# Lane attention: scores as one-pass products of 48 stacked rows, split by the projections

## What is computed

```python
def proj(x, W, bias):
    y = x @ W.T + bias
    y = y.reshape(b, s, H, dk, M)                  # H = 16 heads, dk = 16, M = 4 lanes
    return jnp.transpose(y, (0, 2, 1, 3, 4))
qh, kh, vh = proj(q, Wq, bq), proj(k, Wk, bk), proj(v, Wv, bv)

def interfere(x):
    return x + 0.1 * amp[0] * jnp.einsum('bhsdi,hij->bhsdj', x, interference)
qh, kh, vh = (interfere(qh), interfere(kh), interfere(vh))
scores = jnp.einsum('bhqdm,bhkdm->bhqkm', qh, kh) / math.sqrt(dk)
weights = jax.nn.softmax(scores, axis=3)
out = jnp.einsum('bhqkm,bhkdm->bhqdm', weights, vh)
return out @ Wo.T + bo
```

## Time and profile before

| | us |
|---|---|
| three runs | 3400.84, 3404.05, 3405.44 |
| median | 3404.05 |
| span of the profiled execution | 3398.2 |
| TensorE busy in it | 3209.0 (94%) |
| VectorE busy | 1418.4 (42%) |
| ScalarE busy | 893.4 (26%) |
| GpSimd busy | 347.8 (10%) |

### The profile page before, as it was taken

The page is one execution under the profiler, slowest core; times in us unless marked ns, Lnnn a source line. Parts: engine busy times, 40 slices in busy tenths (PEclk is TensorE's granted clock), DMA queues, the critical chain, the costliest instruction groups (busy, mean ns, idle before and its releaser), DMA issues. The chain is left out here.

```text
span 3398.2 us, 52110 instructions
## 1 busy us (share of the span) xinstructions
PE 3209.0 (94%) x20924; PEld 2468.5 (73%) x20924; DVE 1418.4 (42%) x2020; ACT 893.4 (26%) x1233; POOL 347.8 (10%) x304
## 2 busy tenths in 40 slices
PE   7999569998999989999999799999999999999999
PEld 4555437777788866666666688888888888778877
DVE  6888688872200027887786322122221212300000
ACT  3333344332211125555454211111111111200000
POOL 2000000000000012332332101011111010000000
PEclk9999779998999989999999899999999999999999
DMA  6776512212421241221221522222222223643443
GB/s 142 151 153 135 191 59 72 75 63 93 137 74 56 74 136 65 87 92 74 86 87 50 182 96 95 94 100 87 100 89 97 96 92 127 214 144 97 144 139 104
DMA packets 341895, 361.09 MB, mean 106 GB/s; under 512 B 154624, under 2 KB 261744, under 8 KB 339840
## 3 DMA queue, kind: packets, MB, share of 16 engines
q1 hardware_dynamic: 338304, 356.28, 33.3%
q10 hardware_dynamic: 3456, 2.90, 0.3%
HBM read 215.23 MB, written 135.36 MB: 103 GB/s over the span
## 5 line engine op out<-in xcount | busy, mean ns | idle before, releaser
L2338 PE MATMUL g_ps<-g_xs,g_wt 128*128 128x512 f32 x4128 | 950.4, 391 | 0.0
L2338 PEld LDWEIGHTS g_ps<-g_xs,g_wt 128*128 128x128 f32 x4128 | 775.8, 189 | 160.3
L2397 PE MATMUL g_ps<-g_wd,g_h 128*128 128x512 f32 x2016 | 464.2, 393 | 6.8 <-DVE g_act_out L2254 3.5
L2397 PEld LDWEIGHTS g_ps<-g_wd,g_h 128*128 128x128 f32 x2016 | 381.7, 190 | 88.9 <-DMA g_h<-g_hidden 4.3
L2254 DVE SCALAR_TENSOR_TENSOR g_act_out<-g_ps,g_g,g_act_out 128x512 f32<-128x512 f32 (+1 forms) x88 | 66.1, 751 | 672.8 <-ACT g_act_out L2187 672.7
L2187 ACT ACTIVATE g_act_out<-g_ps 128x512 f32<-128x512 f32 (+1 forms) x88 | 52.6, 598 | 634.4 <-PE g_ps L2338 634.4
L1345 PE MATMUL kv_gps<-kv_xh,kv_wh 128*128 128x512 f32 x512 | 202.1, 395 | 1.0 <-DVE kv_xl L1290 1.0
L1345 PE MATMUL kv_gps<-kv_xh,kv_wl 128*128 128x512 f32 x512 | 199.9, 390 | 0.0
L1345 PE MATMUL kv_gps<-kv_xl,kv_wh 128*128 128x512 f32 x512 | 199.6, 390 | 0.0
L1068 PE MATMUL f_gps<-f_xt,f_qwh 128*128 128x256 f32 x1024 | 192.1, 288 | 1.4 <-DVE f_xt L919 1.4
L2127 POOL TENSOR_TENSOR g_wt<-g_raw,g_wt 128x1024 fp32r<-128x1024 f32 x43 | 102.9, 2393 | 854.1 <-ACT g_wt L2164 854.1
(11 more groups left out here) (270 smaller groups left out, 4320.8 us busy)
## 6 DMA issues: line engine op xcount, KB each, us to landing
g_h<-g_hidden SPq DMA_DIRECT2D x176, 256.0 KB, 2.6
g_hidden<-g_h SPq DMA_DIRECT2D x84, 512.0 KB, 2.7
kv<-kv_y SPq DMA_DIRECT2D x16, 1024.0 KB, 5.6
g_down<-g_raw SPq DMA_DIRECT2D x22, 512.0 KB, 2.8
g_raw<-g_down SPq DMA_DIRECT2D x22, 512.0 KB, 4.1
g_raw<-in_L_ffn_gate_w_dram SPq DMA_DIRECT2D x21, 512.0 KB, 3.9
g_raw<-in_L_ffn_up_w_dram SPq DMA_DIRECT2D x21, 512.0 KB, 3.9
g_raw<-in_L_ffn_down_w_dram SPq DMA_DIRECT2D x21, 512.0 KB, 4.0
```

What stands on the lines that cost most here:

```text
L2338: w = pe.matmul(gps[:, c % 2, m, :], wt[m][i][:, l, ks], xs[c][:, r, k, :], start=(k == 0 and a == 0), stop=(k == NK - 1 and a == 2))
L2397: w = pe.matmul(to, tile[:, p % RING, l, cols], wd[f][:, r, os], start=(f == 0 and a == 0), stop=False)
```

## The change

The high part and the rest of keys and queries are made once, in `projections`, and stored so that the lane attention can load them as stacked rows. For a head and a lane there are 48 rows: of the query (high, high, rest), of the key (high, rest, high), 16 each. Their product over the 48 rows is the sum of high by high, high by rest and rest by high, one fp32r matmul of 48 rows by 128 columns for each of the eight score matrices of a chunk, four in each half of the array. Zeroed rows of other lanes are not needed, so `a_km` and GpSimd's work on it go, and so does the tile `um` from which it was made.

In `projections` ScalarE's result of a key chunk is the high part, VectorE makes the rest (`key_rest`). SyncE stores each half of a key block (eight batches) with six DMAs: high, rest, high, each as two of 64 partitions (the two heads), 256 KB in pieces of 512 B. The queries, computed by the stage before, are loaded (0.5 MB a batch), split by ScalarE (`query_high`) and GpSimd, and stored with six DMAs of 64 partitions, one batch in each block, two in blocks 7 and 8. Values keep their single store. ScalarE's wait for the low-rank stacks stands ahead of block 1 instead of at the end. In `lane_attention` SyncE loads a batch's stacked rows with eight DMAs of 48 partitions by 8 KB (two for each pair of chunks).

```diff
-            def store(n, i):
-                wait_apart(sp, S["c1"], (S["ge"], NC * n + NC), (S["out"], 16 * n))
-                sp.dma_start(out.rearrange("b p n t -> n p b t")[n],
-                             y[:, i, :].rearrange("p (b t) -> p b t", t=P)).then_inc(S["out"], 16)
...
+            def store_keys(n, h):
+
+                wait_apart(sp, S["c1"], (S["gl"], NC * n + 2 * h + 2))
+                for j, part in enumerate(COPIES[1]):
+                    for a in range(2):
+                        to = qk[B // 2 * h:B // 2 * h + B // 2].rearrange("b n w a j r t -> n w a j r b t")
+                        sp.dma_start(to[n, 1, a, j], y[64 * a:64 * a + 64, 2 * h + part, :].rearrange("p (b t) -> p b t", t=P)
+                                     ).then_inc(kst[h], 16)
...
+            def store_queries(b, i):
+                wait_apart(sp, S["c1"], (S["ql"], b + 1))
+                for j, part in enumerate(COPIES[0]):
+                    for a in range(2):
+                        to = qk.rearrange("b n w a j r t -> b w a j r n t")
+                        sp.dma_start(to[b, 0, a, j], qs[64 * a:64 * a + 64, part, :].bitcast(F32).rearrange("p (n t) -> p n t", t=P)
+                                     ).then_inc(S["qst"], 16)
+
+            def step(n, i, key, batches):
+                if not isinstance(n, int) or n + 2 < NB:
+                    wait_apart(sp, S["c1"], (S["wld"], 16 * n + 32), (S["wp"], n + 1))
+                    load_w(n + 2, i)
+                for b, at in batches[0:1]:
+                    load_queries(b, at)
+                if key:
+                    store_keys(n, 0)
+                for b, at in batches[0:1]:
+                    store_queries(b, at)
+                for b, at in batches[1:]:
+                    load_queries(b, at)
+                if key:
+                    store_keys(n, 1)
+                for b, at in batches[1:]:
+                    store_queries(b, at)
+                if not key:
+                    store_values(n, i)
...
+            def key_result(n, c):
+                slot_free = [(kst[c // 2], KST * n)] if c % 2 == 0 and not (isinstance(n, int) and n == 0) else []
                 wait_apart(act, S["c1"], (S["g"], NC * n + c + 1), *slot_free)
-                act.activation(y[:, i, bass.ts(c, 512)], gps[:, c, :], ACT.Identity,
+                act.activation(y[:, c // 2 * 2, bass.ts(c % 2, 512)].bitcast(F32R), gps[:, c, :], ACT.Identity,
                                bias=bmix[:, bass.ts(n, 1)]).then_inc(S["ge"], 1)
...
-            with act.Fori(0, NB // 2 - 1) as j:
-                for i in range(2):
-                    weights(2 * j + 2 + i, i)
-                    results(2 * j + 1 + i, 1 - i)
-            results(NB - 1, 1)
             act.wait_ge(S["stacks"], 16 * 3 * len(jobs))
+            middle_blocks(act, step)
+            step(NB - 1, 1, False, ())
...
+            def key_rest(n, c):
+                wait_apart(dve, S["c1"], (S["ge"], NC * n + c + 1))
+                cols = bass.ts(c % 2, 512)
+                dve.scalar_tensor_tensor(out=y[:, c // 2 * 2 + 1, cols].bitcast(F32R), in0=gps[:, c, :], scalar=bmix[:, bass.ts(n, 1)],
+                                         in1=y[:, c // 2 * 2, cols], op0=ALU.add, op1=ALU.subtract).then_inc(S["gl"], 1)
...
+def stacked_loads(sp, tile, qk, b, r, done):
+
+    for a in range(2):
+        src = qk.rearrange("b (r n) w a j (d m) t -> b r a (j d) (n w) (m t)", n=2, m=4)
+        sp.dma_start(tile[64 * a:64 * a + 48].rearrange("p n w t -> p (n w) t").bitcast(F32), src[b, r, a]).then_inc(done, 16)
...
             def scores(b, par, c, sl):
-                pe.wait_ge(S["km"], NK * b + c + 1)
-                if c == 0:
-                    pe.wait_ge(S["ql"], 16 * b + 16)
-                for a in range(2):
-
-                    rows = slice(64 * a, 64 * a + 64)
-                    m = pe.matmul(rflat[:, sl, 512 * a:512 * a + 512], q[par][rows, c, :],
-                                  km[rows, c % 2, :, :].rearrange("p m t -> p (m t)"), start=True, stop=True)
+                if c % 2 == 0:
+                    pe.wait_ge(qkl[c // 2], 32 * b + 32)
+                tile = qk[c // 2]
+                for h in range(M):
+                    for a in range(2):
+
+                        rows = slice(64 * a, 64 * a + 3 * HD)
+                        m = pe.matmul(ring[:, sl, M * a + h, :], tile[rows, c % 2, 0, P * h:P * h + P],
+                                      tile[rows, c % 2, 1, P * h:P * h + P], start=True, stop=True)
                 m.then_inc(S["s"], 1)
```

More of the change, by code:

```diff
@@ L1207, in _ @@
+            sp.wait_ge(S["out"], 16 * NK)
+            sp.wait_ge(S["stacks"], 16 * 3 * len(jobs))
+            sp.dma_start(early["v"], values[0]).then_inc(E["vl"], 16)
         @block.gpsimd
@@ L1219, in _, with step @@
                                pattern=[[M, P // M], [0, M]], channel_multiplier=-1).then_inc(S["c1"], 1)
+            def step(n, i, key, batches):
+                for b, at in batches:
+                    pool.wait_ge(S["qh"], b + 1)
+                    pool.tensor_tensor(qs[:, 1, :], x[:, at, :], qs[:, 0, :], ALU.subtract).then_inc(S["ql"], 1)
+            middle_blocks(pool, step)
         @block.scalar
@@ L1295, in weights, with step @@
                 dve.tensor_tensor(wl[i][:, :, :], wps[:, :, :], wh[i][:, :, :], ALU.subtract).then_inc(S["wl"], 1)
+            def key_rest(n, c):
[3 more added lines that the diff above has]
+                                         in1=y[:, c // 2 * 2, cols], op0=ALU.add, op1=ALU.subtract).then_inc(S["gl"], 1)
+            def step(n, i, key, batches):
+                weights(n + 1, 1 - i)
+                for c in range(NC):
+                    if key:
+                        key_rest(n, c)
             rest(0)
@@ L1300, in _ @@
                 rest(c)
[L1301 removed]
+                if c == NC - 1:
+                    weights(1, 1)
+                key_rest(0, c - 1)
+            key_rest(0, NC - 1)
             dve.wait_ge(S["high"], 1)
             dve.tensor_tensor(parts[:, 1, :], factors[:, :], parts[:, 0, :], ALU.subtract).then_inc(S["low"], 1)
[L1304 to L1306 removed]
+            middle_blocks(dve, step)
         @block.tensor
@@ L1358, in _, with step @@
             m.then_inc(S["bp"], 1)
-            products(0, 0)
-            with pe.Fori(0, NB // 2 - 1) as j:
-                for i in range(2):
-                    weights(2 * j + 2 + i, i)
-                    products(2 * j + 1 + i, 1 - i)
-            products(NB - 1, 1)
+            def step(n, i, key, batches):
+                weights(n + 1, 1 - i)
+                products(n, i, key)
+            products(0, 0, True)
+            middle_blocks(pe, step)
+            products(NB - 1, 1, False)
+def stacked_loads(sp, tile, qk, b, r, done):
+    for a in range(2):
+        src = qk.rearrange("b (r n) w a j (d m) t -> b r a (j d) (n w) (m t)", n=2, m=4)
+        sp.dma_start(tile[64 * a:64 * a + 48].rearrange("p n w t -> p (n w) t").bitcast(F32), src[b, r, a]).then_inc(done, 16)
 def lane_tiles(nc, ctx, columns):
```

203 lines of the change are left out of this document (119 added, 84 removed).

## The result

| | before | after |
|---|---|---|
| median of the runs, us | 3402.45 | 3426.73 |
| lowest and highest | 3396.52, 3405.44 | 3417.29, 3427.64 |
| span of the profiled execution | 3398.2 | 3415.6 |

The changed kernel is slower: the ratio is 1.0071, with an interval from 1.0053 to 1.0089. The forecast was 3421 us, added up from the median of three runs of before, 3404.05; with the fourth it is 3402.45. What follows is worked out from the trace; what the other three runs lost beyond it is not shown.

What follows compares the result with a forecast made beforehand. TensorE was taken to bound the projections, with VectorE 0.08 to 0.19 us behind it in a lane chunk. The sum was 3404 - 4 (scores) + 0 + 0 + 21 (stores) = 3421 us, range 3395 to 3444.

Steps and rivals of the forecast that it cites:

- the lane: Lane attention: shorter scores bring each chunk down to VectorE's beat, -4 us over the loop's twelve batches, -9 at best.
- the halves overlapping in the products: Lane attention scores: eight products overlap in the array's two halves, taking 0.51 us a chunk instead of 1.06.
- GpSimd's work off the path in the loop: Lane attention: GpSimd's masked products are off the path in the loop, so removing them gains nothing there.
- the forecast's sum of +17: Whole kernel: -4 us from scores and +21 from stores, other terms 0, taking 3404 to 3421 us.
- ScalarE's wait: Projections, ahead of block 1: the wait for the stacks ends about 913 us, in time; cost 0, up to +4 us.
- the first batch: Start of lane attention: about 2 us back from GpSimd, Wo's fifth block some 2 us late; 0, between -2 and +3.
- The stores' term: Projections: key and query stores of 64 partitions at 204 GB/s delay TensorE's weights, about +21 us; bounds 0 to 35.
- step 7: Projections, block with two query batches: 24 stores and three loads take 35.2 us, 11.7 over the beat.
- Rival 1: Projections: half-width stores run above 232 GB/s and stay hidden; 3400 us, or 3393 with larger gains; chance 0.27.
- the 3428 worked out from 196 GB/s: Projections' stores at the skill's rate, 1.34 us each: a term of about 28 us, kernel time 3428 us.
- the slack: Projections: weights asked for 23.6 us early have 12 us to spare, set against a 33 us backlog.
- rival 2: Projections: stores at 188 GB/s cost +35 us, kernel 3442; 3445 with 3 us at TensorE's lower clock; chance 0.11.

Runs made afterwards that it cites:

- halves in a row: Changed kernel with three stores of one half of the partitions, then three of the other, instead of in turn: 3439.3 us.

## Why the prediction was right, and where it was not

**Right**: slower, by a pause in the projections of about the size given (+21 forecast; 19.5 in the trace behind the key half, and 6.2 near the start that have another cause), worst at the weights of blocks 9 and 10 by the forecast, of blocks 10 and 11 by the mixings; the lane faster by little, since VectorE stands right behind TensorE; the halves overlapping in the products (0.60 us against 0.51); GpSimd's work off the path in the loop. That the forecast's sum of +17 is also the trace's 17.4 is luck: the lane gave 9.7 more than its term, while ScalarE's wait, the first batch and the first and last stretch cost 11.6.

**The stores' term was right for a reason that holds only in part.** I took 204 GB/s; the trace has 251. By my own sum the stores would have been hidden from 232 on: at 251 (1.04 us a store) a key block fits, step 7 is 5.9 over, and with the stacks' 6.4 and 12 us to spare nothing is left of the +21. Rival 1's mechanism, that stores of the two halves overlap, is what the halves in a row show. So that the pause came out near 21 is luck, of two errors that made up for each other; so is that the 3428 worked out from 196 GB/s lies near the median. The second error is the slack. I gave the load of weights 12 us to spare and let the backlog come from the queue alone. In the trace a key step of SyncE takes about 23.6 us, the beat itself, with 2.4 us of waiting for the query split in it that I had not counted; it never makes up for the late start in block 1, and at block 9's load only 2.6 us are left. Then block 7 is over by 8.7 (I had 11.7, at the lower rate) and block 8 by 8.5, where I had counted stores and loads only, 12 stores in 32 us. There the term is SyncE's order: 17.7 us from the issue of the two batches' loads to their stores. 8.7 + 8.5 - 2.6 = 14.6 us is about what TensorE waits in the trace (13.8); the other 5.7 of the late pause are work at half the clock, which only rival 2 had, at 3 us.

**ScalarE's wait** was put at 0, up to 4; it is the 6.2 us of the early pause. I had its end at about 913, so that cast and rest, 2.2 us, would reach TensorE before 916.7. It ended at 915.62, and the next mixing came at 918.14, only 0.6 late; I had followed nothing but these weights. Queued behind the wait were block 1's results as well, and behind those six stores and the tile: ScalarE waits 8.00 us more at 929.32.

**The lane** was put at -4, down to -9; it is -13.7 in all. Of the batch's chunks only three intervals stood at 3.02 before, where I counted four; after, one is 2.94 and two are 2.83 and 2.84, the beat that batch 1 showed, so the lower value was the better one. And 0.26 us a batch came from the output projection, which I had said would not move. The loop's twelve batches make 9.5 of the 13.7, the last batch 2.2 (29.8 to 27.6); in the kernels whose lane code is that of the changed one it takes 27.6 to 29.5, so that part may be chance.

**The first batch** was put at 0, -2 to +3; it is +1.9 in this trace and up to +7 in others of the same order.

The Trainium skill (SBUF — State Buffer, "Door 1: The DMA port swizzle" and "Can I just issue two DMAs to hit both halves?") gave 196 GB/s for a transfer of 1 MiB from 64 partitions and 6% more for two transfers at once. In this case's runs the first microsecond of a store from an empty queue makes 166, three stores of a half in a row give 210, and halves in turn 251: a fifth more than in a row, and not 6%. Where they differ the measurement holds. That full width is best, as it also says, the runs show: 287 GB/s.

## What to carry to other kernels

A transfer of half the partitions that fits into the beat by its bytes can still take away the room by which a queue catches up, so write down the in-order step of the issuing engine, waits included, and hold that against the beat. Where the same engine loads, waits for a split and stores, load ahead and keep urgent loads out from behind bulk; here that turned +0.7% into -0.4%. When a wait is moved forward, follow everything that is queued behind it, not only the next instruction.

## What was not expected of the hardware

Stores of 64 partitions alternating between the two halves run at 251 GB/s and three by three at 210, with the same bytes and addresses; the queue's share was near 1 in both. The 48 matmuls of the output projection start 0.235 us apart in the loop of the kernel before and 0.229 in every kernel with stacked rows, at a granted clock of 1.00 in the batches shown of both; nothing that was tried explains it.
